# Output projection of the first layer in f16 halves, with scales made on the chip

## The chip, the core and the metric

The kernel runs on one core of one Trainium2 chip. The metric is the device time of one launch in microseconds (us). TensorE is PE in what follows, its weight loads PEld, VectorE is DVE, ScalarE is ACT, GpSimd is POOL and SyncE is SP; in this kernel SP issues all the transfers (DMA) of the part that is changed. Each engine works through its own list of instructions in order, and semaphores tie the lists together.

## The reference, cut to what matters

Three residual layers with a layer norm behind each. Only the first is touched: a short convolution over time, a long one with a kernel as long as the sequence, a gate, and the output projection. Sizes there: 16 time steps, 256 batch rows, 512 channels, all f32.

```python
up = jnp.einsum('lbd,ed->lbe', xn, W_in) + b_in               # xn: layer norm of x, no gain
uc = short_conv(up, short_w) + short_b                        # 3 taps, each channel by itself
x0, x1, v = jnp.split(uc, 3, axis=1)
v = v * x1
y = long_conv(v, k) + v * conv_bias[None, :, None]            # by FFT in the reference
y = y * x0                                                    # the mixed values
y = jnp.einsum('bld,ed->ble', y, W_out)                       # the output projection
x = _layernorm(x + y, axis=-1)                                # x1, which the later layers read
```

## The kernel before

**Stages.** The batch is taken in two halves of 128 rows (`hf` 0 and 1). A half has 24 *slots* (s = 0 to 23) and then 16 *output blocks* (R = 0 to 15 in the first half, 16 to 31 in the second), one for each time step. The 512 channels are four groups of 128 (`cc` 0 to 3), and a slot is one of three kinds (X1, V, X0) of one group for eight of the 16 steps.

**A slot** goes through three engines. PE makes the input projection in f16 halves: 24 matmuls of 128x512 into one of two banks (L574), high times high, low times high, high times low. ACT reads the bank twice, into `u` (L761) and, times the last tap, into `conv_all` (L769). DVE adds the other two taps (L906); a V slot has a product with X1 behind it (L913). ACT may write `u` again only when DVE is done with the slot that read it.

**The long convolution** of a group (`convolve`, L595) is 16 f32 matmuls on PE with a block Toeplitz matrix, behind slots 7, 13, 18 and 22. What it reads is stored by SP to memory and brought back in another layout; its result goes through ACT (`copy_conv`) and again through memory into the tile `y`. `make_y` (L920) then multiplies four tiles of 128x512 of `y` by X0 on DVE: behind slots 9 and 15, half each behind 20 and 21, and the last group's behind the loop.

**An output block** (`out_part`, L616) is four f32 matmuls of 128x512, one for each group, which the profile counts as eight instructions. DVE adds the residual (L926), takes the statistics (L928, L930), POOL makes the reciprocal root, DVE normalises (L935), and SP stores the block (L321) and loads the residual of a block that is seven further on (L316); that load waits for the store of the block that had the buffer, of eight. Blocks 0 to 3 of a half have the first three groups done for all of them before the fourth group. Between the first half's blocks stand the transposes and splits of the second half's x. `LATE` = 8: the second half's last eight blocks do not stand in this loop. Seven of them are threaded into the start of the *heads*, the second layer, from 434 us on.

**In the first half's slots** much is prepared beside them. DVE takes the row maxima of the next group of input weights (`measure_w_in`, L973 to L988, behind slots 1, 6, 11), PE turns the weights (behind slots 4, 9, 14), ACT copies their high halves, DVE takes the low halves ahead of slots 4, 9 and 14 (`split_w_lo`, L993). The output weights are turned on PE behind slot 5, and ACT copies them into `wout_t` as f32 (`copy_w_out`). POOL has the reciprocal roots and little else.

**In the second half's slots** ACT squares eight parts of the feed-forward weights (L800, behind slots 1, 3, 5 and so on), each waiting for a load, and rounds some of them (L814). A row maximum is taken on DVE behind slot 6, turned on PE behind slot 9, reduced on DVE behind slot 10 (L1029) and spread by a small matmul behind slot 11 (L668).

**The order** on each engine is written out by hand: loops over slots, with tables that say behind which slot a piece of other work goes.

```python
SQUARE_AT = {1: 0, 3: 1, 5: 2, 8: 3, 10: 4, 12: 5, 15: 6, 17: 7}
TURN_AT = {4: 1, 9: 2, 14: 3}
MEASURE_AT = {1: 1, 6: 2, 11: 3}
```

SP too has one list: a load that waits holds every transfer behind it.

## Time and profile before

| | |
|---|---|
| time, median of 3 runs | 997.69 us (995.42 to 998.8) |
| the profiled execution | 998.75 us, of which the span is 997.0 us |
| PE busy | 937.2 us, 94% of the span |
| DVE busy | 816.0 us, 82% |
| ACT busy | 632.5 us, 63% |
| POOL busy | 543.1 us, 54% |
| first half's slots, to about | 188 us |
| first half's output blocks, to about | 266 us |
| second half's slots, to about | 403 us |
| heads and what is behind them | 430 us to the end |

The stage times are read from the timelines of PE and SP. In a row of a timeline stand the start and the length in us, the engine, the line, the operation, what it writes and reads, the count, and in brackets the idle time of the engine ahead of it with what ended that. A row of the chain of waits has start, length, and what was on the chain. Busy shares are means over stages that have different limits, so they say little about any one stage.

### The profile page before, as it was taken

Reading aid. Unit: us, or ns where it says so; the run is one execution under the profiler, and the core shown is the slowest. Engines: PE = TensorE matmul, PEld = TensorE weight load, DVE = VectorE, ACT = ScalarE, POOL = GpSimd, SP = SyncE. Lnnn points to the kernel's source line nnn. Section 1 sums busy time; section 2 is a strip of 40 time slices with the busy share of each in tenths; the row PEclk is TensorE's granted clock in tenths of the full one; section 3 lists DMA queues with packets and bytes.
Section 4 is the critical chain, followed back from the end, with each engine's and each line's share of the span. In section 5 each row is a group of like instructions: output and inputs, shape, how many; then the busy total and the mean of one; then the engine's idle time right before and its main releaser. Section 6 shows DMA issues by size and latency. Waiting matters only on the chain.

```text
span 997.0 us, 14896 instructions
## 1 busy us (share of the span) xinstructions
PE 937.2 (94%) x4490; PEld 545.7 (55%) x4490; DVE 816.0 (82%) x1650; ACT 632.5 (63%) x783; POOL 543.1 (54%) x823
## 2 busy tenths in 40 slices
PE   3989999899889999989999999999999999999985
PEld 2545544555335544445566666666666666666641
DVE  6877986399357476687999999999999999999982
ACT  4756545332356565761577777877777787777774
POOL 5302310033100000157888989889898989889851
PEclk9999999899999999999999999999999999999998
DMA  9235677456756657876386876757575665758433
GB/s 320 56 90 154 191 241 234 157 179 205 235 175 211 191 199 253 279 200 198 109 174 135 160 157 137 178 121 182 129 170 142 150 162 130 177 121 188 84 74 85
DMA packets 210268, 167.86 MB, mean 168 GB/s; under 512 B 125861, under 2 KB 166857, under 8 KB 208169
## 3 DMA queue, kind: packets, MB, share of 16 engines
q1 hardware_dynamic: 210216, 167.24, 61.9%
q8 instruction: 25, 0.41, 0.2%
q14 instruction: 27, 0.21, 0.1%
HBM read 112.36 MB, written 33.87 MB: 147 GB/s over the span
## 4 chain that ended last, share of the span: by engine, by line
PE 66%; DVE 14%; DMA 9%; ACT 5%; issue 4%; SPq 2%; DVEq 0%; POOL 0%; POOLq 0%; ACTq 0%
PE conv_bank L1549 17%; PE slot_bank L574 14%; PE hq_bank L1635 11%; PE conv_bank L1559 6%; PE back_bank L1656 4%; PE ff_bank L1656 4%; DMA x_scratch<-res 4%; PE slot_bank L616 4%; DVE conv_all L906 3%; PE conv_bank L595 3%; PE back_bank L1624 1%; PE back_bank L1544 1%; DMA v_ct<-v_scratch 1%; ACT conv_all L769 1%; DVE x_lo L894 1%
## 5 line engine op out<-in xcount | busy, mean ns | idle before, releaser
L906 DVE SCALAR_TENSOR_TENSOR conv_all<-u,taps,conv_all 128x1024 f32<-128x1024 f32 x92 | 122.4, 1331 | 104.2 <-ACT conv_all L769 102.4
L2002 POOL TENSOR_TENSOR sum<-z 128x512 f32<-128x512 f32 x128 | 162.9, 1273 | 23.6 <-DVE z L1865 23.6
L1635 PE MATMUL hq_bank<-x_lo,hq_t 128*128 128x512 f16 x512 | 121.9, 383 | 4.0 <-DMA hq_t<-hq_int 4.0
L616 PE MATMUL slot_bank<-wout_t,y 128*128 128x512 f32 x256 | 114.0, 600 | 3.7 <-DVE res L926 3.7
L761 ACT ACTIVATE u<-slot_bank,bias,unscale 128x1024 f32<-128x1024 f32 x46 | 55.4, 1205 | 94.5 <-PE slot_bank L574 68.7
L2006 POOL TENSOR_TENSOR sum<-sum 128x256 f32<-128x256 f32 x128 | 94.7, 740 | 10.0
L574 PE MATMUL slot_bank<-x_hi,w_hi 128*128 128x512 f16 x384 | 93.1, 385 | 7.5 <-ACT conv_all L769 5.9
L574 PE MATMUL slot_bank<-x_lo,w_hi 128*128 128x512 f16 x384 | 92.5, 383 | 3.0 <-DVE x_lo L894 3.0
L574 PE MATMUL slot_bank<-x_hi,w_lo 128*128 128x512 f16 x384 | 91.9, 382 | 0.0
L1744 ACT ACTIVATE hq_f<-g,h_scale 128x1024 f32<-128x1024 f32 x64 | 73.2, 1144 | 23.5 <-DVE h_scale L1913 19.5
L1918 DVE TENSOR_REDUCE g_max<-g 128x1 f32<-128x512 f32 x128 | 83.9, 676 | 4.8 <-ACT g L1783 4.8
L1549 PE MATMUL conv_bank<-block_diag 128*128 128x288 f32 x324 | 86.4, 407 | 0.1
L1865 DVE TENSOR_TENSOR z<-conv_bank,qx 128x512 f32<-128x512 f32 x128 | 86.3, 674 | 0.0
L1549 PE MATMUL conv_bank<-kv,block_diag 128*128 128x288 f32 x320 | 85.6, 406 | 0.6 <-ACT conv_bank L1735 0.6
L1635 PEld LDWEIGHTS hq_bank<-x_lo,hq_t 128*128 128x128 f16 x512 | 50.4, 99 | 59.6 <-DMA hq_t<-hq_int 4.5
L1168 POOL TENSOR_SCALAR r_rstd<-r_meanvar 128x1 f32<-128x1 f32 x32 | 18.5, 578 | 115.9 <-DVE r_meanvar L930 115.9
L616 PEld LDWEIGHTS slot_bank<-wout_t,y 128*128 128x128 f32 x256 | 48.6, 193 | 60.3 <-issue 55.4
L1559 PE MATMUL conv_bank<-kv_hi,block_diag 128*128 128x288 f16 x376 | 77.0, 286 | 1.2 <-DVE z L1865 0.9
L1852 DVE TENSOR_TENSOR z<-conv_bank,qx 128x384 f32<-128x384 f32 x128 | 70.0, 547 | 0.0
L1549 PEld LDWEIGHTS conv_bank<-block_diag 128*128 128x128 f32 x324 | 60.3, 190 | 17.6 <-issue 0.6
L1549 PEld LDWEIGHTS conv_bank<-kv,block_diag 128*128 128x128 f32 x320 | 59.6, 190 | 17.9 <-ACT conv_bank L1735 1.1
L1656 PE MATMUL ff_bank<-x_hi,xq_t 128*128 128x512 f16 x256 | 65.8, 379 | 3.2 <-ACT g L1783 2.0
(203 smaller groups left out, 1930.1 us busy)
## 6 DMA issues: line engine op xcount, KB each, us to landing
block_diag<-in_ctx_turned SPq DMA_DIRECT2D x32, 512.0 KB, 3.8
x_quad<-in_w_t SPq DMA_DIRECT2D x10, 1024.0 KB, 7.7
stage<-in_ctx SPq DMA_DIRECT2D x16, 512.0 KB, 6.6
v_scratch<-conv_all SPq DMA_DIRECT2D x16, 512.0 KB, 4.1
c_scratch<-v_tok SPq DMA_DIRECT2D x8, 1024.0 KB, 5.3
y<-c_scratch SPq DMA_DIRECT2D x8, 1024.0 KB, 4.9
res<-in_x SPq DMA_DIRECT2D x32, 256.0 KB, 3.2
x_scratch<-res SPq DMA_DIRECT2D x32, 256.0 KB, 3.3
```

Source lines behind the costliest of these rows:

```text
L574: last = nc.tensor.matmul(slot_bank[n % 2][:, q, :], wt[:, dc, e * P:(e + 1) * P], xt[:, dc, cols], start=(j == 0 and dc == 0), stop=(j == ...
L616: last = nc.tensor.matmul(out_bank(R), y[:, cc, t, :], w["wout_t"][:, cc, :], start=(cc == 0), stop=(cc == DC - 1))
L906: ins = nc.vector.scalar_tensor_tensor(out=acc, in0=(u_first[kind] if n < 3 else u)[:, t0 + tap:t0 + tap + T // 2, :].rearrange("p t b -> ...
L1549: last = nc.tensor.matmul(view(conv_bank[tb % 2][:, hh, :], 0, (ROW64, T // 2), (1, PAIRS)), toep[:, head.buf, window * P:(window + 1) * P ...
L1559: last = nc.tensor.matmul(view(conv_bank[tb % 2][:, hh, :], 0, (ROW64, T // 2), (1, PAIRS)), toep_half[:, head.buf, (part * HALVES + windo ...
L1635: last = nc.tensor.matmul(hq_bank[:, :], hq_t[:, fc, :], w["w2_t"][:, fc, :], start=(fc == 0), stop=(fc == FC - 1))
L1656: last = nc.tensor.matmul(bank[:, :], xq_t[:, dc, :], w["w1_t"][:, dc, k * 512:(k + 1) * 512], start=(dc == 0), stop=(dc == DC - 1))
L1744: nc.scalar.activation(hq_f[:, half], g[:, half], ACT.Copy, scale=h_scale[:, 0:1], bias=LOW_HALF).then_inc(hq_rounded, 1)
L1865: nc.vector.tensor_tensor(view(z[:, b, :, :], 0, (SEGS * SEG, T), (2 * SEG + 1, 4), (1, HD)), view(conv, 0, (ROW64, T), (HD, 4), (1, HD)), ...
L1918: nc.vector.tensor_reduce(g_max[:, k:k + 1], g[:, k * 512:(k + 1) * 512], AX_X, ALU.max, apply_absolute_value=True).then_inc(g_maxed, 1)
L2002: nc.gpsimd.tensor_tensor(sum2[:, :, :].rearrange("p t (s j) -> p t s j", j=HD), view(z[:, b, :, :], 0, (SEGS * SEG, T), (SEG, half), (1, ...
L2006: nc.gpsimd.tensor_tensor(sum1[:, :, :], sum2[:, :, 0:2 * HD], sum2[:, :, 2 * HD:4 * HD], ALU.add).then_inc(sum1_done, 1)
```

## The change

The output projection is made from f16 halves. The mixed values are multiplied by a power of two for each channel and split into a high and a low f16 part; the output weights are multiplied by the inverse of that, times one common power of two, and split as well. A block is then three passes of f16 matmuls (high by high, high by low, low by high), 12 instructions of 128x512 in place of 8, and the add of the residual undoes the common scale in the same instruction.

The scale of a channel comes from a bound on its largest value, made in the first half: the sum of the absolute taps and of the absolute long kernel, the sum of the squares of each row of the input weights (`square_rows`), the biases, and a root on POOL. Then the largest of the scaled output weights over all channels is needed, which goes over partitions: DVE takes a maximum for each partition (`top_of_w_out`), PE turns it into a row, DVE takes the row's maximum, PE spreads it with a matmul, DVE makes the scales.

New instructions, beside those that only change their form:

- **Setup, DVE:** five small operations on kernel sums and taps (in `long_kernels`), and `square_rows(0)`, three multiplies of 128x512 with an accumulator, ahead of the first low halves of the weights.
- **First half, DVE:** `square_rows` and `bound_y` (nine small ones) behind slots 4, 6, 8 and 13 (group 0's squares are in the setup), `scale_y` (three small) behind 5, 7, 9 and 14; `top_of_w_out` behind 14, `out_row_of` behind 16, `out_scales` behind 17, `w_out_lo` (four of 128x512) behind 19.
- **First half, PE:** a transpose of the maximum behind slot 15 and a small matmul behind slot 16; the convolution of group 2 waits for the scales. **POOL:** four roots. **ACT:** `w_out_hi`, four copies of 128x512 behind slot 18. **SP:** the load of `y` of group 3 waits for the halves of the output weights, since the turned f32 weights now stand in that part of `y`.
- **Both halves:** `make_y` writes the scaled product into `conv_all`; ACT copies it to f16 (`y_hi`), DVE subtracts that for the low part (`y_lo`), four tiles each, behind slots 9, 16, 21, 22 and the loop. ACT's next X0 slot, and the projection, wait for `y_lo`.
- Some semaphores become one (`rms_steps`, `res_agg`), with the same order of events.

The diff, cut to its core:

```diff
+    BOUND_AT = {4: 0, 6: 1, 8: 2, 13: 3}
+    Y_SCALE_AT = {5: 0, 7: 1, 9: 2, 14: 3}
+    OUT_TOP_AT, TURN_OUT_AT, OUT_ROW_AT, SPREAD_OUT_AT, OUT_SCALE_AT, OUT_HI_AT, OUT_LO_AT = 14, 15, 16, 16, 17, 18, 19
+
+    HI_AT = {9: (0, range(4)), 16: (1, range(4)), 21: (2, range(2)), 22: (2, range(2, 4))}
+    LO_AT = HI_AT
...
+            if k == DC - 1:
+                sp.wait_ge(wout_steps, 13)
...
             for cc in ccs:
-                last = nc.tensor.matmul(out_bank(R), y[:, cc, t, :], w["wout_t"][:, cc, :],
-                                        start=(cc == 0), stop=(cc == DC - 1))
+                for i, (rows, cols) in enumerate(((0, 0), (0, 1), (1, 0))):
+                    last = nc.tensor.matmul(out_bank(R), y_half(cc, t // QUAD, rows, t % QUAD * P, P), wout_half[cols][:, cc, :],
+                                            start=(cc == 0 and i == 0), stop=(cc == DC - 1 and i == 2))
...
+        def turn_out_top():
+
+            pe.wait_ge(wout_steps, 1)
+            pe.wait_ge(ch_copied, 4 * 2)
+            nc.tensor.transpose(turn_bank[3][0:1, 0, :], out_top[:, :], w["ident"][:, :]).then_inc(wout_steps, 1)
+
+        def spread_out_top():
+
+            pe.wait_ge(wout_steps, 3)
+            nc.tensor.matmul(turn_bank[3][:, 1, 0:1], ones[0:1, :], out_row[:, :], start=True, stop=True).then_inc(wout_steps, 1)
...
-                        others = [(w_lo_done, KINDS * (cc + 2))] + [(wout_done, DC)] * (cc == 0)
+                        others = [(w_lo_done, KINDS * (cc + 2))] + [(wout_done, DC)] * (cc == 0) + [(wout_steps, 5)] * (cc == 2)
...
-                act.wait_ge(y_done, 4 * ck - 2 + 2 * pr)
+                act.wait_ge(y_lo_done, 4 * ck - 2 + 2 * pr)
...
+        def w_out_hi():
+
+            act.wait_ge(k_stored, 16)
+            act.wait_ge(wout_steps, 5)
+            for cc in range(DC):
+                nc.scalar.activation(wout_half[0][:, cc, :], wout_f[:, cc, :], ACT.Copy, scale=out_scale[:, cc:cc + 1]).then_inc(wout_steps, 1)
+
+        def y_hi(hf, cc, ks):
+            for k in ks:
+                act.wait_ge(y_done, 4 * (hf * DC + cc) + k + 1)
+                nc.scalar.copy(y_half(cc, k, 0), conv[X0][:, 4 * k:4 * k + 4, :].rearrange("p t b -> p (t b)")).then_inc(y_hi_done, 1)
...
-                out = y[:, cc, 4 * k:4 * k + 4, :]
+                x0 = conv[X0][:, 4 * k:4 * k + 4, :].rearrange("p t b -> p (t b)")
                 dve.wait_ge(c_loaded, 16 * (hf * DC + cc + 1))
-                nc.vector.tensor_tensor(out, out, conv[X0][:, 4 * k:4 * k + 4, :], ALU.mult).then_inc(y_done, 1)
+                nc.vector.scalar_tensor_tensor(out=x0, in0=y[:, cc, 4 * k:4 * k + 4, :].rearrange("p t b -> p (t b)"),
+                                               scalar=y_scale[:, cc:cc + 1], in1=x0, op0=ALU.mult, op1=ALU.mult).then_inc(y_done, 1)
+
+        def y_lo(hf, cc, ks):
+            for k in ks:
+                dve.wait_ge(y_hi_done, 4 * (hf * DC + cc) + k + 1)
+                nc.vector.tensor_tensor(y_half(cc, k, 1), conv[X0][:, 4 * k:4 * k + 4, :].rearrange("p t b -> p (t b)"), y_half(cc, k, 0),
+                                        ALU.subtract).then_inc(y_lo_done, 1)
...
-            nc.vector.tensor_tensor(res[:, i, :], out_bank(R), res[:, i, :], ALU.add).then_inc(res_added, 1)
+            nc.vector.scalar_tensor_tensor(out=res[:, i, :], in0=out_bank(R), scalar=out_unscale[:, 0:1], in1=res[:, i, :],
+                                           op0=ALU.mult, op1=ALU.add).then_inc(res_added, 1)
...
+        def square_rows(i):
+
+            dve.wait_ge(win_scaled, KINDS * (i + 1))
+            for e in range(i * KINDS, (i + 1) * KINDS):
+                link(nc.vector.scalar_tensor_tensor(out=w["wout_t"][:, 0, :], in0=raw_w_in(e), scalar=w["unscale"][:, e:e + 1], in1=raw_w_in(e),
+                                                    op0=ALU.mult, op1=ALU.mult, accum_out=row_squares[:, e:e + 1]))
+
+        def bound_y(i):
+
+            part = slice(i * KINDS, (i + 1) * KINDS)
+            square_of(bias_square[:, part], w["bias"][:, part], REST)
+            link(nc.vector.tensor_tensor(bound[:, part], row_squares[:, part], w["unscale"][:, part], ALU.mult))
+            link(nc.vector.scalar_tensor_tensor(out=bound[:, part], in0=bound[:, part], scalar=MOST * D, in1=bias_square[:, part],
+                                                op0=ALU.mult, op1=ALU.add))
+            link(nc.vector.tensor_tensor(bound[:, part], bound[:, part], tap_sum[:, part], ALU.mult))
+            link(nc.vector.tensor_tensor(bound[:, part], bound[:, part], short_square[:, part], ALU.add))
+            first, second, third = (bound[:, i * KINDS + k:i * KINDS + k + 1] for k in range(KINDS))
+            out = y_bound[:, i:i + 1]
+            link(nc.vector.tensor_tensor(out, first, kernel_sum[:, i:i + 1], ALU.mult))
+            link(nc.vector.tensor_tensor(out, out, second, ALU.mult))
+            link(nc.vector.tensor_tensor(out, out, third, ALU.mult))
+            nc.vector.tensor_scalar(out, out, LEAST, None, ALU.max).then_inc(y_bounds, 1)
...
+        def top_of_w_out():
+
+            dve.wait_ge(wout_done, DC)
+            link(nc.vector.tensor_reduce(out_max[:, :], wout_f, AX_X, ALU.max, apply_absolute_value=True))
+            link(nc.vector.tensor_tensor(out_max[:, :], out_max[:, :], y_pow2[:, :], ALU.mult))
+            nc.vector.tensor_reduce(out_top[:, :], out_max[:, :], AX_X, ALU.max).then_inc(wout_steps, 1)
+
+        def out_row_of():
+
+            dve.wait_ge(wout_steps, 2)
+            nc.vector.tensor_reduce(out_row[:, :], turn_bank[3][0:1, 0, :], AX_X, ALU.max).then_inc(wout_steps, 1)
...
+        def root_of_bound(i):
+            pool.wait_ge(y_bounds, 2 * i + 1)
+            nc.gpsimd.tensor_tensor(y_bound[:, i:i + 1], y_bound[:, i:i + 1], w["neg_half"][:, 0:1], ALU.pow).then_inc(y_bounds, 1)
```

**PE behind slots 15 and 16 of the first half.** Each slot is four rows here, 24 matmuls. Before:

```order
L574 MATMUL slot_bank1<-x_hi,w_lo 128x512 x8
L574 MATMUL slot_bank0<-x_hi,w_hi 128x512 [waits tap2_done,w_lo_done]
L574 MATMUL slot_bank0<-x_hi,w_hi 128x512 x7
L574 MATMUL slot_bank0<-x_lo,w_hi 128x512 x8
L574 MATMUL slot_bank0<-x_hi,w_lo 128x512 x8
L574 MATMUL slot_bank1<-x_hi,w_hi 128x512 [waits tap2_done]
L574 MATMUL slot_bank1<-x_hi,w_hi 128x512 x7
```

Now, with line numbers of the changed kernel:

```order
L611 MATMUL slot_bank1<-x_hi,w_lo 128x512 x8
L694 MATMUL conv_bank1<-ident,out_top 1x128 [waits ch_copied,wout_steps]
L611 MATMUL slot_bank0<-x_hi,w_hi 128x512 [waits tap2_done,w_lo_done]
L611 MATMUL slot_bank0<-x_hi,w_hi 128x512 x7
L611 MATMUL slot_bank0<-x_lo,w_hi 128x512 x8
L611 MATMUL slot_bank0<-x_hi,w_lo 128x512 x8
L699 MATMUL conv_bank1<-out_row,ones 128x1 [waits wout_steps]
L611 MATMUL slot_bank1<-x_hi,w_hi 128x512 [waits tap2_done]
L611 MATMUL slot_bank1<-x_hi,w_hi 128x512 x7
```

The transpose of the maximum (L694) stands between slots 15 and 16, the matmul that spreads it (L699) between 16 and 17, and each waits for a step that DVE makes.

**DVE around slots 13 to 15 of the first half.** Before, from the taps of slot 13 on:

```order
L906 SCALAR_TENSOR_TENSOR conv_all<-u,taps,conv_all 128x1024 [waits tap2_done]
L906 SCALAR_TENSOR_TENSOR conv_all<-u,taps,conv_all 128x1024 [waits tap1_done]
L993 TENSOR_TENSOR w_lo<-conv_bank,w_hi 128x4x128 [waits w_hi_done] x3
L906 SCALAR_TENSOR_TENSOR conv_all<-u,taps,conv_all 128x1024 [waits tap2_done]
L906 SCALAR_TENSOR_TENSOR conv_all<-u,taps,conv_all 128x1024 [waits tap1_done]
L913 TENSOR_TENSOR conv_all<-conv_all 128x1024 [waits conv_done]
L885 TENSOR_SCALAR x_quad<-x_quad,meanvar,rstd 128x512 [waits x_rstd]
```

Now, from the low halves ahead of slot 14 on (ahead of them there are twelve new instructions behind slot 13, squares and bound):

```order
L1070 TENSOR_TENSOR w_lo<-conv_bank,w_hi 128x4x128 [waits w_hi_done] x3
L975 SCALAR_TENSOR_TENSOR conv_all<-u,taps,conv_all 128x1024 [waits tap2_done]
L975 SCALAR_TENSOR_TENSOR conv_all<-u,taps,conv_all 128x1024 [waits tap1_done]
L982 TENSOR_TENSOR conv_all<-conv_all 128x1024 [waits conv_done]
L1117 TENSOR_SCALAR y_scale<-y_bound 128x1 [waits y_bounds]
L1118 TENSOR_SCALAR y_scale<-y_scale 128x1 [waits setup_chain]
L1119 RECIPROCAL y_pow<-y_scale 128x1 [waits setup_chain]
L1124 TENSOR_REDUCE out_max<-y 128x4 [waits wout_done,setup_chain]
L1125 TENSOR_TENSOR out_max<-out_max,y_pow 128x4 [waits setup_chain]
L1126 TENSOR_REDUCE out_top<-out_max 128x1 [waits setup_chain]
L954 TENSOR_SCALAR x_quad<-x_quad,meanvar,rstd 128x512 [waits x_rstd]
```

The maximum over the output weights (L1124 to L1126) stands behind slot 14's product; L694 on PE waits for the last of these. The normalisation of x (L885, now L954) stands behind it.

**DVE at slot 16 of the first half.** Before:

```order
L906 SCALAR_TENSOR_TENSOR conv_all<-u,taps,conv_all 128x1024 [waits tap2_done]
L906 SCALAR_TENSOR_TENSOR conv_all<-u,taps,conv_all 128x1024 [waits tap1_done]
L876 BN_STATS stats<-x_quad 128x6 [waits x_loaded1]
L876 BN_STATS stats<-x_quad 128x6 x3
L879 BN_AGGR meanvar<-stats 128x2 [waits x_stats] x4
```

Now:

```order
L975 SCALAR_TENSOR_TENSOR conv_all<-u,taps,conv_all 128x1024 [waits tap2_done]
L975 SCALAR_TENSOR_TENSOR conv_all<-u,taps,conv_all 128x1024 [waits tap1_done]
L1131 TENSOR_REDUCE out_row<-conv_bank 1x1 [waits wout_steps]
L995 TENSOR_TENSOR y<-conv_all,y 128x512 [waits y_hi_done] x4
L945 BN_STATS stats<-x_quad 128x6 [waits x_loaded1]
```

The row's maximum (L1131), for which L699 on PE waits, stands behind both taps of slot 16, and the four subtractions of group 1 stand behind it.

## Rows read from the trace of the kernel before

**Rows 1.** Chain of waits in order of time: start us, length us, what.

```profile
210.22 3.62 DMA x_scratch<-res
...
446.47 3.43 PE slot_bank L616 x8
...
512.55 1.73 PE hq_bank L1635 x8
```

**Rows 2.** Timeline of DVE, setup: start, length, what, count, idle ahead.

```profile
12.05 0.69 DVE L953 SCALAR_TENSOR_TENSOR block_diag<-x_quad,block_diag 128x512 f32<-128x512 f32 x1
...
18.88 0.17 DVE L973 TENSOR_SCALAR row_max<-row_max 128x3 f32<-128x3 f32 x1
19.08 0.17 DVE L974 TENSOR_SCALAR row_pow<-row_max 128x3 uint32<-128x3 uint32 x1
...
19.82 2.47 DVE L894 TENSOR_TENSOR x_lo<-conv_bank,x_hi 128x512 f16<-128x512 f32 x4
...
24.41 0.16 DVE L986 TENSOR_TENSOR tap_scale<-unscale,taps 128x3 f32<-128x3 f32 x1
24.49 0.15 DVE L987 TENSOR_TENSOR tap_bias<-bias,taps 128x3 f32<-128x3 f32 x1
...
29.85 2.48 DVE L894 TENSOR_TENSOR x_lo<-conv_bank,x_hi 128x512 f16<-128x512 f32 x4 [2.35 <-ACT x_hi L741]
```

**Rows 3.** Windows, DVE: stretch, length, busy (count), clock, DMA share, GB/s.

```profile
57.00:95.00 38.00, 25.79 (x34) 1.00 0.28 76
95.00:133.00 38.00, 35.10 (x50) 1.00 0.71 222
```

**Rows 4.** Timeline of DVE, first half.

```profile
92.38 2.60 DVE L906 SCALAR_TENSOR_TENSOR conv_all<-u,taps,conv_all 128x1024 f32<-128x1024 f32 x2 [5.19 <-ACT conv_all L769]
...
133.07 1.91 DVE L885 TENSOR_SCALAR x_quad<-x_quad,meanvar,rstd 128x512 f32<-128x512 f32 x4
...
137.53 1.23 DVE L913 TENSOR_TENSOR conv_all<-conv_all 128x1024 f32<-128x1024 f32 x1
...
162.43 1.22 DVE L913 TENSOR_TENSOR conv_all<-conv_all 128x1024 f32<-128x1024 f32 x1
...
199.82 0.69 DVE L926 TENSOR_TENSOR res<-slot_bank,res 128x512 f32<-128x512 f32 x1 [2.70 <-PE slot_bank L616]
```

**Rows 5.** Timeline of PE, first half's slots and convolutions.

```profile
54.62 1.04 PE L574 MATMUL slot_bank<-x_lo,w_hi 128*128 128x512 f16 x4 [3.03 <-DVE x_lo L894]
...
131.34 1.89 PE L574 MATMUL slot_bank<-x_hi,w_hi 128*128 128x512 f16 x8
...
136.52 1.89 PE L574 MATMUL slot_bank<-x_hi,w_hi 128*128 128x512 f16 x8
...
148.40 3.84 PE L595 MATMUL conv_bank<-v_ct,block_diag 128*128 128x128 f32 x32 [1.36 <-DMA v_ct<-v_scratch]
...
177.15 6.29 PE L595 MATMUL conv_bank<-v_ct,block_diag 128*128 128x128 f32 x32 [4.20 <-issue]
```

**Rows 6.** Timelines of PE and DVE: slot 21's end, its taps.

```profile
167.61 1.89 PE L574 MATMUL slot_bank<-x_hi,w_hi 128*128 128x512 f16 x8
...
170.15 2.61 DVE L906 SCALAR_TENSOR_TENSOR conv_all<-u,taps,conv_all 128x1024 f32<-128x1024 f32 x2 [1.24 <-ACT conv_all L769]
```

**Rows 7.** Timelines of ACT and PE, second half's slots.

```profile
273.12 1.91 ACT L800 ACTIVATE x_quad<-x_quad 128x2048 f32<-128x2048 f32 x1 [8.24 <-DMA x_quad<-in_w_t]
...
325.69 0.38 PE L668 MATMUL conv_bank<-top_diag,ones 2*128 2x2 f32 x2 [1.34 <-DVE top_diag L1029]
```

**Rows 8.** Timelines, heads' start; last, a window: PE, PEld, DVE, ACT, POOL.

```profile
432.36 2.00 ACT L814 ACTIVATE conv_all<-conv_all,rms 128x2048 f32<-128x2048 f32 x1 [3.13 <-DMA conv_all<-in_w_t]
...
434.13 0.68 DVE L926 TENSOR_TENSOR res<-slot_bank,res 128x512 f32<-128x512 f32 x1
...
434.87 5.40 PE L616 MATMUL slot_bank<-wout_t,y 128*128 128x512 f32 x8 [3.66 <-DVE res L926]
...
443.00:486.00 43.00, 42.85 (x156) 24.76 (x155) 36.32 (x76) 8.26 (x11) 33.32 (x47) 1.00 0.57 168
```

More of the change, by code:

```diff
@@ L859, in scalar_part @@
                     round_part(ROUND_AT[s])
+            y_hi(hf, DC - 1, range(4))
             if hf + 1 < HALF:
@@ L1072, in vector_part @@
         split_lo(0)
+        square_rows(0)
         split_w_lo(0)
@@ L1121, in vector_part @@
             make_y(hf, DC - 1, range(4))
+            y_lo(hf, DC - 1, range(4))
             if not more:
```

137 lines of the change are left out of this document (111 added, 26 removed).

## Prediction

> **What bounds the kernel now.** I read the chain of waits first, for what sets the end in each stretch; then the windows, for how much room VectorE (DVE) has; then the timelines of PE, DVE and ACT around the places that the change touches. The kernel has three kinds of stretch. From 430 us on the heads run, with PE full; the change touches only their start, where seven blocks of the output projection are threaded in. In each half of the batch there are 24 "slots" (input projection and short convolution: 5.18 us of PE, then two ACT steps, then two DVE steps), and behind them 16 output blocks.
>
> Three facts decide. First, one output block is 3.43 us of PE, and eight f16 matmuls of the same size take 1.73, so 12 take 2.59: 0.84 less for each of 32 blocks [rows 1]. Second, in the first half's blocks the chain is not PE but the stores, one behind the other (3.62 each); they hold the next loads on SP, and ACT later sits idle 8.24 us for such a load [rows 1, 7]. Third, in the first half's slots DVE has 12.2 us free in 57–95, but only 2.9 in 95–133 [rows 3]. That is where the change puts its new work.
>
> **Part 1: what PE gives back.** 32 x 0.84 = 26.9 us of PE, but only part is on the path. The first half's blocks are paced by the stores: block 0's add on DVE waited 2.70 for PE [rows 4], and the four new subtractions of the last channel group (2.47 for four [rows 2]) fill just that wait, so the first store leaves as before. I take -1 (ends -3, 0). The second half's first eight blocks end in a wait of PE for DVE (3.66 [rows 8]), so their gain is lost there. The seven late blocks stand in a stretch where PE is busy 42.85 of 43 us and DVE 36.3 [rows 8]: at most -5.9. DVE then has about 1 us of room left, so I take -5 (ends -5.9, -2).
>
> **Part 2: new DVE work in the first half.** Prices [rows 2]: a 128x512 multiply with an accumulator 0.69, with the wait for itself 0.75; small operations that wait for one another 0.20 apart; a subtraction to f16 0.62. So the squares of three weight blocks are 2.25, a bound (nine small ones) 1.8, a scale 0.6, the maximum over 4x512 elements, for which the trace has no row, like a pass of four tiles, 2.5 (1.2 and 4 as ends). The new multiply into conv_all costs what the old one did. The ACT copies of y follow it tile by tile and are priced where they hold something up.
>
> Step 1. The squares of the first weight block (2.25) fit in an idle of 2.35 [rows 2]. The kernel sums (five small operations, 1.0) do not: PE already waits 3.03 us for x_lo behind them [rows 5]. +1.0.
>
> Step 2. Ahead of slot 7, DVE gets bound, scale, squares and bound: 6.5. With step 1 and less 1.4 of idle it ends slot 7 at 93.3 instead of 87.2; the idle of 5.19 ahead of slot 8 [rows 4] is used up. ACT may not overwrite u for slot 8 before, and needs 2.4; slot 8 starts on DVE at 95.8 instead of 92.38: +3.4.
>
> Step 3. From there to 133.07 DVE gets squares and bound twice (8.1), four subtractions (2.5) and a scale (0.6), 11.2, against 2.4 of idle. +12.2: the end of the work at slot 14 moves from 133.07 [rows 4] to 145.3. Then the last scale and the maximum over the output weights: 3.5 with its two small operations. The top is ready at 148.8.
>
> Step 4. **PE waits for it.** The transpose of that maximum stands on PE behind slot 15, which ended at 131.34 [rows 5], and slot 16 stands behind it. PE gets later on the way too (slot 12 now waits for ACT, which waits for the subtractions), by some 9 us, but that is inside this wait. Slot 16 starts at 149.0: +17.7.
>
> Step 5. **A whole round trip is put between two slots.** The matmul that spreads the maximum stands on PE behind slot 16 and waits for a DVE operation that stands behind DVE's part of the same slot 16. From the end of a slot on PE to the end of its DVE part is 167.61 to 172.76, 5.15 [rows 6]; with the reduction (0.3) and the matmul with its hops (0.4, as at 325.69 [rows 7]) PE stands 5.9. Slot 17 starts at 149.0 + 5.2 + 5.9 = 160.1 instead of 136.52 [rows 5]: +23.5. The convolution of channel group 2 then waits for the scales (slot 17's end, 5.15, and six small operations, 1.2): 171.7 instead of 148.40, where it had waited anyway: +23.3.
>
> Step 6. Some comes back. In the trace the convolution of group 3 begins 13.5 us behind its product (163.65 to 177.15 [rows 4, 5]), after a wait of 4.20, and then takes 6.29 where the one before took 3.84; group 2's began 9.6 behind its product (138.76 to 148.40). Now the product is ready at 187.0, PE arrives at 196.1, and the convolution begins at 196.6 to 200.5, at 3.84 without the long wait. The first half's slots end +17 to +23.3 later; I take +19.5, nearer to the shorter way, because the loads that slowed this one are issued earlier relative to it. Wider ends, for DVE prices that I have wrong by a fifth: +11 and +25. Nothing that I see on SP makes this up, since all of the first half's loads and stores move with it.
>
> A row of the trace against a page: small DVE operations that wait for one another start 0.20 apart (18.88, 19.08), and two that do not, 0.08 (24.41, 24.49) [rows 2]. The Trainium skill, page "VectorE: DVE Perf Modes", section "The DRAIN you can't avoid", says that a semaphore between operations costs nothing extra; it measured that on large copies. By that rule some 50 small operations would be 0.1 cheaper, and the time about 5 us lower, near 1012. The row decides here.
>
> **Part 3: the second half and the start of the heads.** ACT's copies of y stand behind slot 9 and wait for the multiply; four subtractions (2.5) stand ahead of DVE's slot 10. The row maximum behind that slot comes 2.9 later, and PE, which had waited 1.34 for it [rows 7], stands that much longer: +2.9 (ends 0, +4.5). The other subtractions there fall into idle of DVE. At the end ACT holds its rounding back until the last copy of y (6 us), and DVE has 2.5 more ahead of its adds. The add at 434.13, which releases PE at 434.87 after 3.66 of waiting, moves by about 3; ACT's idle of 3.13 at 432.36 [rows 8] takes up most of its own delay. PE's next blocks are 0.8 shorter. +2.4 (ends 0, +4).
>
> **Sum,** against the profiled execution's own 998.75 us (span 997.0; the median of the runs shown is 997.69, 1.06 lower): +19.5 - 1 + 2.9 + 2.4 - 5 = +18.8, so 1017.6; less part of that 1.06, I say 1017.
>
> **Rivals.** (a) PE sets the end everywhere, as its busy share suggests: -26.9, 972 us. The stores and the waits on DVE [rows 1, 4, 8] speak against it. The Trainium skill, page "FP8 and Floating Point Precision", section "TensorE Precision Notes", counts four passes for a full f32 product, so three f16 passes save a quarter; the trace agrees on the passes (0.857 against 0.216). It gives this time only where PE is what ends last.
> (b) Faster: the new work in the first half falls into DVE's idle. DVE has 15 us free in 57–133 and more later, against 19 ahead of the top of the output weights; if PE and ACT let DVE run ahead, so that the maximum is there when slot 15 ends and the row maximum when slot 16 ends, the first half costs nothing. Then -1 - 5 + 2.9 + 2.4 gives 998, and 993 if part 3 is hidden as well. The point is the top of the output weights being ready at 131; the trace puts the last product ahead of it at 133.07 without any new work. That speaks against it.
> (c) Steps 2 and 3 are absorbed, and only the two trips remain: the top at 133.07 + 3.5, so +5.3, then +5.9, less some 3 at group 3's convolution: +8 in place of 19.5, 1006 us.
> (d) The change does not do what it says: f16 matmuls whose weights change each time do not run at 0.216 as those of the heads do. The late blocks then give nothing: 1022.
>
> **How the numbers follow.** About 0.3% is what a measurement of this kernel can tell from no change. Forecast, with (d) inside it, 0.70, own range 1010 to 1027; (c) 0.14; (b) at 998 0.06, at 993 0.07; (a) 0.03. So faster 0.10, same 0.06, slower 0.84. The range must hold 8 in 10: 1004 to 1027 takes in (c) and the ends of the unknown costs above it; (a) and (b) are left out.
>
> **What would show it.** In the profile after: the transpose of the output maximum on PE with a wait of some 8 us on DVE, and the matmul behind it with 5 to 6; DVE nearly full from slot 8 to slot 16; the first block's add some 17 us later than 199.82; the gap between the first and last store unchanged; the late blocks at 2.6 us. I am wrong if DVE's reduction over the output weights starts before 140, or if the stores move closer together, since then the first half's blocks give their gain after all.

## The result, and the profile after

The changed kernel takes 1023.0 us (median of 4 runs, 1021.78 to 1024.67), the kernel before 997.41 in the same comparison: a ratio of 1.0244, with a 95% interval of 1.0213 to 1.0275. The profiled execution took 1022.74 us against 998.75, +24.0; its span is 1020.9 us against 997.0, +23.9. The first line of the page after, busy time and share of the span by engine:

```profile
PE 926.8 (91%) x4621; PEld 539.4 (53%) x4621; DVE 862.9 (85%) x1773; ACT 652.5 (64%) x819; POOL 542.8 (53%) x827
```

PE's busy time fell by only 10 us: the matmuls of the blocks take 26.5 us less (114.0 before, 87.5 after), but those of the slots take 10.5 more (277.5 and 288.0), since some of them now ran at half clock. DVE's busy time rose by 47. The blocks are as cheap as they should be. The chain of waits after (start, length, what), to be held against [rows 1]:

```profile
233.48 3.14 DMA x_scratch<-res
...
477.76 2.59 PE slot_bank L654 x12
```

A block takes 2.59 us of PE instead of 3.43: f16 matmuls with changing weights do run at 0.216. The time is lost in the first half. Its timeline of PE:

```profile
55.55 1.45 PE L611 MATMUL slot_bank<-x_lo,w_hi 128*128 128x512 f16 x4 [3.84 <-DVE x_lo L963]
...
115.18 3.57 PE L611 MATMUL slot_bank<-x_hi,w_hi 128*128 128x512 f16 x8 [6.66 <-ACT conv_all L822]
...
148.61 0.37 PE L694 MATMUL conv_bank<-ident,out_top 128*1 128x128 f32 x1 [4.87 <-DVE out_top L1126]
148.78 3.29 PE L611 MATMUL slot_bank<-x_hi,w_hi 128*128 128x512 f16 x8
...
160.75 0.58 PE L699 MATMUL conv_bank<-out_row,ones 1*128 1x1 f32 x2 [5.22 <-DVE out_row L1131]
161.26 3.60 PE L611 MATMUL slot_bank<-x_hi,w_hi 128*128 128x512 f16 x8
...
174.67 3.81 PE L632 MATMUL conv_bank<-v_ct,block_diag 128*128 128x128 f32 x32 [0.91 <-DVE out_scale L1141]
...
201.44 5.44 PE L632 MATMUL conv_bank<-v_ct,block_diag 128*128 128x128 f32 x32 [2.25 <-issue]
```

Three waits for DVE, directly or through ACT, stand where the kernel before has none: 6.66 at slot 12, 4.87 at the transpose of the maximum, 5.22 at the small matmul. Behind each, the first eight matmuls take 3.3 to 3.6 us instead of 1.89. DVE at the places that the prediction named, in its timeline:

```profile
96.20 2.60 DVE L975 SCALAR_TENSOR_TENSOR conv_all<-u,taps,conv_all 128x1024 f32<-128x1024 f32 x2 [2.05 <-ACT conv_all L822]
...
148.40 0.16 DVE L1126 TENSOR_REDUCE out_top<-out_max 128x1 f32<-128x4 f32 x1
...
160.42 0.27 DVE L1131 TENSOR_REDUCE out_row<-conv_bank 1x1 f32<-1x128 f32 x1
...
222.62 0.75 DVE L1002 SCALAR_TENSOR_TENSOR res<-slot_bank,out_unscale,res 128x512 f32<-128x512 f32 x1
```

Its windows, as in [rows 3] (busy, count, granted clock of TensorE, DMA share, GB/s):

```profile
57.00:95.00 38.00, 29.58 (x62) 0.97 0.23 71
95.00:133.00 38.00, 35.83 (x63) 0.87 0.52 170
```

The first add is 22.8 us later than in [rows 4], and nearly all of the change stands there already. This is how the delay against before runs through the program, from the two timelines:

| place | before | after | delay |
|---|---|---|---|
| first half: first add on DVE | 199.82 | 222.62 | +22.8 |
| second half: ACT's first squared part | 273.12 | 295.80 | +22.7 |
| second half: the small matmul behind slot 11 | 325.69 | 349.75 | +24.1 |
| heads: first late block | 434.87 | 459.54 | +24.7 |
| heads: just behind the last late block | 484.08 | 505.15 | +21.1 |
| heads: 10 us further on | 494.11 | 518.10 | +24.0 |
| end of the span | 997.0 | 1020.9 | +23.9 |

### The profile page after: what moved, and what is told of

It is laid out like the page before. It is cut to its first block, busy times and chain, and to the rows that moved or that the text cites. A ratio compares the mean times of both kernels' runs of the same rounds, so it can differ in the third digit from the quotient of the medians.

```text
span 1020.9 us, 15328 instructions
## 1 busy us (share of the span) xinstructions
PE 926.8 (91%) x4621; PEld 539.4 (53%) x4621; DVE 862.9 (85%) x1773; ACT 652.5 (64%) x819; POOL 542.8 (53%) x827
## 4 chain that ended last, share of the span: by engine, by line
PE 57%; DVE 22%; DMA 6%; ACT 4%; issue 3%; SPq 0%; DVEq 0%; POOL 0%; POOLq 0%; ACTq 0%
PE conv_bank L1727 16%; PE slot_bank L611 11%; PE hq_bank L1813 10%; PE conv_bank L1737 6%; DVE conv_all L975 5%; PE back_bank L1834 4%; PE ff_bank L1834 4%; DMA x_scratch<-res 3%; PE conv_bank L632 2%; DVE r_stats L1005 2%; DVE res L1002 1%; PE back_bank L1802 1%; PE back_bank L1722 1%; ACT u L814 1%; DVE z L2043 1%
## 5 line engine op out<-in xcount | busy, mean ns | idle before, releaser
L611 PE MATMUL slot_bank<-x_hi,w_hi 128*128 128x512 f16 x384 | 100.2, 407 | 13.2 <-ACT conv_all L822 11.6
L611 PE MATMUL slot_bank<-x_lo,w_hi 128*128 128x512 f16 x384 | 95.0, 391 | 3.9 <-DVE x_lo L963 3.8
L654 PE MATMUL slot_bank<-wout_t,y 128*128 128x512 f16 x384 | 87.5, 384 | 8.4 <-DVE res L1002 6.6
L1338 POOL TENSOR_SCALAR r_rstd<-r_meanvar 128x1 f32<-128x1 f32 x32 | 18.6, 582 | 120.0 <-DVE r_meanvar L1007 120.0
L611 PEld LDWEIGHTS slot_bank<-x_hi,w_hi 128*128 128x128 f16 x384 | 39.0, 103 | 60.9 <-issue 18.2
L1727 PEld LDWEIGHTS conv_bank<-block_diag 128*128 128x128 f32 x324 | 60.3, 190 | 18.6 <-issue 1.4
L1834 PE MATMUL back_bank<-x_hi,xq_t 128*128 128x512 f16 x256 | 66.1, 381 | 3.5 <-DVE x L2055 3.0
```

The lines of the kernel that those rows point to most:

```text
L611: last = nc.tensor.matmul(slot_bank[n % 2][:, q, :], wt[:, dc, e * P:(e + 1) * P], xt[:, dc, cols], start=(j == 0 and dc == 0), stop=(j == ...
L654: last = nc.tensor.matmul(out_bank(R), y_half(cc, t // QUAD, rows, t % QUAD * P, P), wout_half[cols][:, cc, :], start=(cc == 0 and i == 0) ...
L1727: last = nc.tensor.matmul(view(conv_bank[tb % 2][:, hh, :], 0, (ROW64, T // 2), (1, PAIRS)), toep[:, head.buf, window * P:(window + 1) * P ...
L1834: last = nc.tensor.matmul(bank[:, :], xq_t[:, dc, :], w["w1_t"][:, dc, k * 512:(k + 1) * 512], start=(dc == 0), stop=(dc == DC - 1))
```

## Experiments

Ratios are to the kernel before, with 95% intervals; 0.1% is 1 us. A trace is one execution. Kernels whose code is the same up to the first add have that add up to 1.9 us apart (222.62, 222.96 and 224.50 in the changed kernel, with the store first and with one late pass), so a smaller difference there says little.

### The bound left out

```diff
-        square_rows(0)
-                    if s in BOUND_AT: ...            # and all steps up to out_scales
+        nc.gpsimd.memset(y_scale[:, :], 1.0)
+        nc.gpsimd.memset(out_scale[:, :], 1024.0)
```

> This kernel is the changed one with the bound left out: no sums, squares, roots, no maximum over the output weights and no trip over PE; the scales are fixed powers of two (1 for the mixed values, 1024 for the weights) set by POOL at the start. The f16 halves and the three passes stay. Theory (the bound's work on DVE and its two trips cost the first half's +23.4 us, the halves themselves little): the first add of a block lies within 0 to 3 us of the 199.82 of before, the second half adds 1 to 2, the late blocks give nothing, so 998 to 1004 us. Rival 1 (the copies and subtractions of the halves are what costs): 1012 us or more. Rival 2 (without the bound the 27 us that PE saves come through): 972 to 985 us.

Measured: 1.0058 (1.0036 to 1.0081), about +5.8 us. Three quarters of the loss, 18.6 of 24.4 us, is the bound with its trips; the rest is the halves' own work. Rival 1 falls, since it wanted 1012 us or more, and so does rival 2: without the bound the 27 us of PE still do not come through. The first add stands at 205.00, +5.2, more than the 0 to 3 that I gave it.

### The low part left out as well

```diff
         def y_lo(hf, cc, ks):
-            for k in ks: ...
+            pass
-                for i, (rows, cols) in enumerate(((0, 0), (0, 1), (1, 0))):
+                for i, (rows, cols) in enumerate(((0, 0), (0, 1), (0, 0))):
```

> Fixed scales with the low part of the mixed values left out: no subtractions on DVE (40 in all), and the third pass repeats the first, so that PE's work is the same. Theory (what the halves themselves cost, 5.8 us, is these subtractions in front of DVE's slots and adds): 4 to 7 us less than fixed scales, 996 to 1000. Rival (ACT's copies or the longer add cost it): 1002 to 1005.

Measured: 0.9989 (0.9970 to 1.0007), 6.9 us less than fixed scales: the subtractions on DVE, and the waits for them, are what the halves cost. They are 32, four tiles for each of four groups in both halves, and not 40. The waits of PE, ACT and SP that stood on them now stand on ACT's copies. With the subtractions gone the kernel is where it was, and still not 27 us faster.

### The trip one slot later

```diff
-    OUT_TOP_AT, TURN_OUT_AT, OUT_ROW_AT, SPREAD_OUT_AT, ... = 14, 15, 16, 16, 17, 18, 19
+    OUT_TOP_AT, TURN_OUT_AT, OUT_ROW_AT, SPREAD_OUT_AT, ... = 14, 16, 16, 17, 17, 18, 19
```

> The transpose of the output maximum stands on PE behind slot 16 instead of 15, and the matmul that spreads it behind 17 instead of 16; everything else as in the changed kernel. Theory (PE's two waits, 4.87 and 5.22 us, and the slots at half clock behind them, 1.4 and 1.9 us more, are on the path): both waits go, slot 17 ends near 155 instead of 168.4, and the time falls by 9 to 13 us, to 1010 to 1014. Rival (DVE is so far behind that it sets the end of the slots with or without the trips): a fall of 0 to 3 us, 1020 us or more.

Measured: 1.0153 (1.0120 to 1.0187), 9 us less. But only one wait went. Its timeline of PE:

```profile
148.92 0.27 PE L694 MATMUL conv_bank<-ident,out_top 128*1 128x128 f32 x1
...
159.71 0.58 PE L699 MATMUL conv_bank<-out_row,ones 1*128 1x1 f32 x2 [5.34 <-DVE out_row L1131]
```

The transpose no longer waits. The small matmul does as before, because DVE comes to the row's maximum only behind its part of slot 16, and that was 10.8 us behind the transpose. So the time agreed with the theory for a reason that was half of what I said. In the trace the first add comes 5.7 us earlier (216.93), the first wait and what it did to the clock; the rest of the 9 is inside the interval. The traced execution, 1019.32 us, was the longest of its six.

### The waits filled

```diff
         def turn_out_top():
+            for _ in range(45):
+                nc.tensor.matmul(turn_bank[0][:, 0:2, :]..., w["w_hi"][:, 0, 0:P], x_hi[:, 0, 0:2 * P], start=True, stop=True)
             pe.wait_ge(wout_steps, 1)
...
         def spread_out_top():
+            for _ in range(48):                      # the same matmul
             pe.wait_ge(wout_steps, 3)
```

> The changed kernel with idle PE filled: 45 matmuls of 128x256 into a free bank ahead of the transpose of the output maximum (its wait was 4.87 us), and 48 ahead of the small matmul that spreads it (5.22 us). They use nothing of the result and nothing waits for them. Theory (part of the price of the two waits is that PE runs at the lower clock behind each: slots 16 and 17 took 6.6 and 7.1 us instead of 5.18): both slots go back to 5.2 to 5.4, and the time falls by 2 to 4 us, to 1019 to 1021. Rival (the waits themselves are the whole price, DVE gives the pace behind them): no change, 1023.

Windows of PE over slot 16 and slot 17 (stretch, length, busy, granted clock, DMA share, GB/s), of the changed kernel:

```profile
148.70:155.40 6.70, 6.70 (x25) 0.78 0.05 16
161.20:168.40 7.20, 7.20 (x25) 0.72 0.84 303
```

and with the waits filled:

```profile
148.70:154.00 5.30, 5.30 (x26) 1.00 0.00 0
159.90:165.10 5.20, 5.20 (x26) 1.00 1.05 381
```

The granted clock was 0.78 and 0.72 behind an idle PE, so part of each slot ran at the lower of its two levels (1.2 GHz); behind a busy PE it was 1.00, the higher one (2.4 GHz), and both slots took 5.2 us. Slot 12, where nothing was edited, took 6.6 us here and 8.0 in the changed kernel, behind the same wait of 6.66: what a wait costs behind it differs between executions. The convolution of group 2 began at 171.39 instead of 174.67, 3.3 earlier, and group 3's and the first add (220.36) 1.9 and 2.3 earlier. The time, 1.0226 (1.0198 to 1.0255), lies 1.8 us under the changed kernel's, which the intervals don't tell from nothing. The clock's part of the delay is shown in the trace at group 2's convolution, not in the time.

### The bound taken off DVE, and the trip moved on DVE too

```diff
+        def square_w(i):                             # ACT, blocks 1 to 3, ahead of their scaling
+                nc.scalar.activation(w["wout_t"][...], raw_w_in(e), ACT.Square, accum_out=row_squares[:, e:e + 1])
...
+            after(nc.gpsimd.tensor_tensor(bound[:, part], bound[:, part], tap_sum[:, part], ALU.mult))
+            ...                                      # POOL: the small operations of bound_y
```

> The changed kernel with the bound kept but taken off DVE: the squares of the weight blocks 1 to 3 on ACT (ahead of their scaling), the small operations of the bound on POOL; and the transpose and the small matmul one slot later, as in the second run. DVE keeps the squares of block 0, the kernel sums, the scales, the maximum over the output weights. Theory (what is left of the first half's delay after the two waits is DVE's queue): within 1 to 5 us of fixed scales, 1005 to 1009. Rival (the rest of the delay is the halves' own work or the trips): 1013 to 1017, as with the two steps moved alone.

Measured: 1.0107 (1.0080 to 1.0134), 4.6 us less than the trip moved alone and 4.9 above fixed scales. Its interval and that of the trip moved alone overlap; in the trace the first add came 3.6 us earlier (213.29), so by the trace what DVE was rid of counts. PE's wait at the small matmul was still 5.34, so the next run moved DVE's steps too:

```diff
-    OUT_TOP_AT, TURN_OUT_AT, OUT_ROW_AT, SPREAD_OUT_AT, OUT_SCALE_AT, ... = 14, 16, 16, 17, 17, 18, 19
+    OUT_TOP_AT, TURN_OUT_AT, OUT_ROW_AT, SPREAD_OUT_AT, OUT_SCALE_AT, ... = 14, 16, 15, 17, 16, 18, 19
```

> As with the bound taken off DVE, and DVE's two steps of the trip also one slot earlier: the row's maximum behind slot 15 instead of 16, the scales behind slot 16 instead of 17 (PE's transpose stays behind slot 16, its small matmul behind 17). There PE still waited 5.34 us at the small matmul and ran slot 18 at half clock, since DVE came to the row's maximum only at the end of its part of slot 16. Theory (with DVE's queue and both waits gone the bound is nearly free): the wait of 5.34 goes, 7 to 9 us less than with the bound taken off DVE, 999 to 1003, at or below fixed scales. Rival (the chain through group 3's convolution takes it back): 1006 to 1009.

Measured: 1.0117 (1.0079 to 1.0156), above the theory's range; the rival's 1006 to 1009 lies in the lower part of the interval. The wait went and the time did not. Its timelines of PE and ACT:

```profile
149.71 0.38 PE L703 MATMUL conv_bank<-out_row,ones 1*128 1x1 f32 x2 [0.18 <-DVE out_row L1147]
...
163.43 1.20 ACT L818 ACTIVATE u<-slot_bank,bias,unscale 128x1024 f32<-128x1024 f32 x1 [8.27 <-DVE conv_all L990]
...
190.08 5.44 PE L636 MATMUL conv_bank<-v_ct,block_diag 128*128 128x128 f32 x32 [5.11 <-issue]
```

And a window of DVE:

```profile
136.80:163.40 26.60, 25.98 (x43) 1.00 0.62 220
```

PE waits 0.18 where it waited 5.34. But DVE is busy 25.98 of 26.60 us, so ACT waits 8.27 for it at slot 18, and PE meets its next wait, 5.11 ahead of group 3's convolution. The first add came 2.3 us earlier only (211.03). An idle PE at the trip was, by this run, room that DVE's queue used anyway.

### The store ahead of the load

```diff
-                if R + RES - 1 < HALF * T:
-                    load_res(R + RES - 1)
                 store_res(R)
+                if R + RES - 1 < HALF * T:
+                    load_res(R + RES - 1)
```

The same edit in the changed kernel, in the kernel before, and with fixed scales:

> On SP the store of block R is issued ahead of the load of the residual of block R + 7, so that a store no longer waits behind a load that waits for the store before it; nothing else differs from the changed kernel. Theory (the first half's blocks are paced by that chain, which is why PE's saving there gives nothing): the stores move closer together, ACT's wait for the first squared part near 290 shortens, and the time falls by 8 to 18 us, to 1005 to 1015. Rival (the chain is only what the profile shows as last, and PE or DVE would take its place at once): 1020 to 1023.

> The kernel before, with the one change of the order on SP: the store of block R ahead of the load of the residual of block R + 7. Theory (the chain of stores paces the first half's blocks and holds the load that ACT waits 8.24 us for): that wait goes, PE's waits of 1.83 and 4.09 us at the start of the second half go with it, 988 to 993 us. Rival (the chain matters only together with the halves): 996 to 999.

> Fixed scales, no bound, f16 halves, and the store ahead of the load on SP. Theory (PE's 13 us in the first half's blocks are hidden by the chain of stores): without the chain they show, so the fall against fixed scales alone is larger than that of the kernel before by the same edit, 8 to 14 us: 990 to 996. Rival (once the chain is gone DVE paces these blocks, and PE's saving stays hidden): the same fall as the kernel before has, so that it stays some 6 us above that kernel with the same edit.

| | load first | store first | difference |
|---|---|---|---|
| before | 1 | 0.9937 (0.9911 to 0.9963) | -6.3 us |
| fixed scales | 1.0058 | 0.9960 (0.9940 to 0.9980) | -9.8 us |
| the change | 1.0244 | 1.0155 (1.0118 to 1.0192) | -8.9 us |

The chain of stores was real. From the first half's first store to its last it is 62.3 us in the kernel before (203.45 to 265.74) and 62.6 after (226.37 to 288.94); with the store first it is 50.6 and 50.5, and 49.9 with fixed scales. SP's timeline of the kernel before, first and last store:

```profile
203.45 0.33 SPq L321 DMA_DIRECT2D x_scratch<-res  x1
...
265.74 0.73 SPq L321 DMA_DIRECT2D x_scratch<-res  x1
```

and with the store first:

```profile
204.25 0.33 SPq L321 DMA_DIRECT2D x_scratch<-res  x1
...
254.80 0.33 SPq L321 DMA_DIRECT2D x_scratch<-res  x1
```

PE's saving still does not show. That the two f16 kernels fall by some 3 us more is about what the intervals leave open, and in the traces the stretch from the first add to the small matmul behind slot 11 of the second half is as long in all three: 117.9 us before, 118.0 with fixed scales, 118.4 with the change (load first: 125.9, 128.1 and 127.1). PE does come to the second half's slots 3 us sooner behind the first add with fixed scales (47.6 us against 50.6), and then waits 3 us longer at that matmul (4.41 against 1.34). What stands next in the blocks is in the windows of the two, f32 before and f16 with fixed scales, store first (busy time of PE, PEld, DVE, ACT, POOL):

```profile
204.00:255.00 51.00, 51.00 (x165) 25.28 (x164) 46.33 (x98) 15.11 (x28) 17.78 (x34) 1.00 0.75 253
```

```profile
207.00:257.50 50.50, 43.83 (x219) 23.52 (x218) 47.10 (x98) 14.74 (x28) 17.89 (x34) 0.93 0.77 253
```

With f32 PE is full; with f16 it is not, the stretch is as long, and DVE is busy 93%. DVE is not alone there: in the f16 kernel's chain of waits DVE's adds come first, then a load of the second half's x, for which DVE waits, and behind that PE is the last again.

```profile
215.25 8.58 DMA x_quad<-in_x
...
234.15 10.36 PE slot_bank L654 x48
```

### The late blocks with one pass

```diff
+                passes = ((0, 0), (0, 1), (1, 0)) if R < HALF * T - LATE else ((0, 0),)
```

> The last eight output blocks leave out two of the three passes (high by low and low by high), so each is 0.86 us of PE instead of 2.59. Theory (DVE, not PE, ends last in the stretch where these blocks stand): a fall of 0 to 2 us, 1021 to 1023. Rival (PE is the bound there, and the gain of the first version was lost elsewhere): seven blocks by 1.73 us, 12 us less, 1011.

Measured: 1.0219 (1.0184 to 1.0254), 2.5 us less, inside the intervals. From the first late block to just behind the last it took 45.53 us, and 45.61 in the changed kernel, though each of the eight blocks was 1.73 us of PE shorter. Windows of the stretch, changed kernel and one pass (PE, PEld, DVE, ACT, POOL):

```profile
467.30:509.00 41.70, 39.43 (x193) 23.61 (x194) 38.51 (x76) 8.14 (x11) 33.12 (x48) 1.00 0.56 165
```

```profile
471.00:512.00 41.00, 31.44 (x131) 20.17 (x132) 38.01 (x76) 8.26 (x11) 32.60 (x47) 0.88 0.56 164
```

PE goes from 95% to 77%, DVE stays at 92 to 93%, and PE waits for DVE more often and longer. The longest of these waits, in the timeline of PE with one pass:

```profile
499.53 0.64 PE L1738 MATMUL conv_bank<-kv_hi,block_diag 128*128 128x288 f16 x2 [3.42 <-DVE z L2044]
```

So DVE ends last here. In [rows 8] it was PE, with 42.85 of 43.

### All delays out

The kernel with the bound off DVE and both trips hidden, the store first, and the second half's small matmul one slot later (`SPREAD_AT` 11 to 12); then the maximum over the output weights behind slot 7 instead of 14, and the halves of these weights two slots later.

```diff
-    TOPS_AT, TURN_TOPS_AT, TOP_ROW_AT, SPREAD_AT, ... = 6, 9, 10, 11, 12, 14
+    TOPS_AT, TURN_TOPS_AT, TOP_ROW_AT, SPREAD_AT, ... = 6, 9, 10, 12, 12, 14
```

> The kernel of the run before this one, with the store ahead of the load on SP, and in the second half the small matmul that spreads the row maxima behind slot 12 instead of 11 (PE waited 4.41 us for it with fixed scales, 1.34 in the kernel before). Theory (the three delays add): 9 us less for the stores and 2 to 4 for the matmul, 987 to 993, faster than the kernel before by 0.5 to 1%. Rival (DVE takes over as soon as the stores and the waits are gone): 994 to 999.

```diff
-    ..., OUT_SCALE_AT, OUT_HI_AT, OUT_LO_AT = 14, 16, 15, 17, 16, 18, 19
+    ..., OUT_SCALE_AT, OUT_HI_AT, OUT_LO_AT = 14, 16, 15, 17, 16, 20, 21
...
+                    if s == 7:
+                        out_max_of()
```

> The kernel of the store-first run with the bound (all delays taken out together), with two steps moved: the maximum over each partition of the output weights, 2.28 us of DVE that needs no scale, from behind slot 14 to behind slot 7, where DVE stood idle 5.4 us; and the halves of the output weights two slots later (ACT behind slot 20, DVE behind 21), since ACT's four copies behind slot 18 kept PE waiting 2.2 us. Theory (moving the trip alone gave nothing because DVE was busy 98% of the time from 137 to 163 us and set the pace there): the first add of a block comes 2 to 5 us earlier than in that run, and the time falls by as much, to 990 to 993. Rival (group 3's trip through memory to its convolution sets the pace): no change, 994 to 996.

Measured: 0.9963 (0.9945 to 0.9981) and 0.9967 (0.9948 to 0.9986). Both beat the kernel before, neither by the 0.5 to 1% expected, and the kernel before with the one edit on SP has the lower ratio, 0.9937; the intervals overlap. In the second, group 3's product came 6.4 us earlier (170.27 against 176.71), its convolution 3.5, the first add 2.5 (208.08 against 210.58): DVE's queue was part of the pace, and the trip from the product through memory to the convolution took the rest back. The time of the two is not told apart.

Behind the first add these two are the fastest of all. From that add to the end of the span it is 784.2 and 784.6 us in their traces, 790.0 with fixed scales, 791.6 with the change and 790.5 with the kernel before, all with the store first. Behind that add they differ from the other two f16 kernels only in the small matmul of the second half, whose wait of 4.41 is gone; the traces put some 6 us on it, but it was not run by itself, and not in the kernel before either. What the change still costs stands ahead of that add: 210.58 and 208.08 against 200.62.

## Why the prediction was right, and where its terms were off

The prediction was 1017, with a range of 1004 to 1027; the time is 1023.0. The main mechanism, DVE's new work and two trips over PE in the first half's slots, is as it said. That the sum came as near is in part luck: terms that were too low by 8.5 us met others that were too high by 3.3. By its own steps:

**The chain of step 1 to step 4 held to a fraction of a microsecond.** PE's first matmul behind `x_lo` began at 55.55 instead of 54.62 [rows 5], +0.9 (said: +1.0). DVE's slot 8 began at 96.20 (said: 95.8), the top of the output weights was ready at 148.56 (148.8), slot 16 began at 148.78 (149.0). PE's wait there was 4.87 where I said some 8: PE had got later by more than the 9 that I allowed, because slot 12 ran in part at half clock behind its own wait of 6.66 (8.0 us instead of 5.18), inside this one.

**Step 5: the waits were right, the slots behind them were not.** The wait was 5.22 (said: 5.9). But I priced slots 16 and 17 at 5.18 each behind idle waits of 5 us, and they took 6.6 and 7.1 at a granted clock of 0.78 and 0.72. Group 2's convolution began at 174.67 instead of 171.7. The filled waits give these 3.3 us back at just this place.

**Step 6 gave back less than I took.** Group 3's convolution began at 201.44, behind the later end of 196.6 to 200.5, and took 5.44, not 3.84; I had chosen +19.5 from 17 to 23.3, and the first add shows +22.8. The way from the product to the convolution was 11.6 us, inside the 9.6 to 13.5 of the rows; the product itself was ready 2.9 us later than said (189.9 instead of 187.0), behind the later convolution of group 2. With the waits filled, 2.3 of the 3.3 us come back at the first add. And 23.3, the end of the range, holds only with the old length of 6.29; with the 3.84 that I wrote beside it, the end would have been 20.9.

**Part 1: the first half's blocks gave nothing, for the reason named.** -1 said, -0.1 in the table. The distance of the stores was unchanged, 4.2 us on average (the 3.62 that I named is one of them), and the edit on SP shows that they were the pace. I had not said what stands right behind them. The second half's first eight blocks gave nothing either, as said: PE's wait for DVE at their end, 3.66 in [rows 8], is longer now.

```profile
459.54 4.07 PE L654 MATMUL slot_bank<-wout_t,y 128*128 128x512 f16 x12 [4.99 <-DVE res L1002]
```

**Part 1: the late blocks are the term whose mechanism failed.** -5 said; -3.6 at the last late block, and 10 us later the delay is +24.0 again, so about 0. The rows, before:

```profile
489.99 1.04 PE L1656 MATMUL back_bank<-x_hi,xq_t 128*128 128x512 f16 x4 [0.69 <-DVE x L1877]
```

and after:

```profile
512.84 1.36 PE L1834 MATMUL back_bank<-x_hi,xq_t 128*128 128x512 f16 x4 [2.22 <-DVE x L2055]
```

PE came early and waited for DVE there. DVE's 36.3 of 43 us [rows 8] looked like room; it was work that had only to fit into 5 us less, and it is in a chain with PE (each group's matmuls, then DVE, then PE). Of the 2.9 us lost again here, 1.5 is that longer wait; some 1.1 more is that the matmuls behind it ran in part at the lower clock (granted 0.68 from 512.80 to 518.10; 4.12 us became 5.26). One pass instead of three left the late blocks' stretch as long as it was (45.53 us).

**Part 3 was too dear.** +2.9 and +2.4 said, +1.4 and +0.6 in the table. PE's wait at the small matmul did grow by 3.07, from 1.34 [rows 7] to 4.41, but PE came to it only 21.0 us later than before, not 22.7. And the reason that I gave for it, the subtractions, is wrong at this place: without them the wait was still 4.40. The rows after, of PE, ACT and DVE:

```profile
349.75 0.58 PE L717 MATMUL conv_bank<-top_diag,ones 2*128 2x2 f32 x2 [4.41 <-DVE top_diag L1175]
```

```profile
341.81 2.60 ACT L860 CAST y<-conv_all 128x512 f16<-128x512 f32 x4 [4.60 <-DVE conv_all L989]
```

```profile
346.65 2.61 DVE L975 SCALAR_TENSOR_TENSOR conv_all<-u,taps,conv_all 128x1024 f32<-128x1024 f32 x2 [0.48 <-ACT conv_all L822]
```

ACT waits 4.60 for DVE's multiply, makes its four copies of `y`, and only then reads slot 10's bank, for which DVE waits; without the subtractions DVE waits for it longer, 2.88, to the same end. No run took the copies away by themselves.

The errors of the terms are +3.3 (slots), +0.9 (first half's blocks), -1.5 and -1.8 (part 3) and +4.3 (late blocks): 5.2 us, from 18.8 to the 24.0 of the profiled executions. The largest is the late blocks.

**The rivals.** (a) falls: with all of the bound gone, the ratio is still 1.0058. (b) falls with the top at 148.56 instead of 131, and (c) with slot 8 at 96.20 and the wait of 6.66 at slot 12. (d) falls with 2.59 us for a block; its 1022 is near the time because it, too, takes nothing for the late blocks, but for another reason. On the row against the page: the bound's small operations, each waiting for the one ahead, did start 0.20 apart in the trace after (102.63, 102.83, 103.03), as [rows 2] had it.

**What PE waits for ahead of group 3's convolution.** The profile names nothing for it ("issue"). It was 2.25 to 7.90 us in these kernels, and from the end of the product on DVE to that convolution it took 11.6 us (after) to 14.6 (early maximum). SP's rows name it: the load of what the convolution reads, its issue and its time from issue to landing, after and with the early maximum:

```profile
195.87 0.70 SPq L372 DMA_DIRECT2D v_ct<-v_scratch  x1
DMA to landing us min/median/max: 5.5/5.5/5.5
```

```profile
180.47 0.70 SPq L376 DMA_DIRECT2D v_ct<-v_scratch  x1
DMA to landing us min/median/max: 5.6/5.6/5.6
```

The load lands at 201.4 and 186.1, and the convolution begins at 201.44 and 186.12. Ahead of its issue SP waits for the stores of the product, 5.4 us after and 7.9 with the early maximum: the load is issued 6.0 us behind the end of the product after, and 9.0 with the early maximum. So it is the trip through memory, and the store is the part of it that differs. Why the store took longer there stays open, and no run shortened the trip.

## What to carry to other kernels

A saving on the engine that is 94% busy was worth next to nothing in three stretches (the blocks of the first half, of the second half, and the late ones): a chain of stores or DVE stood right behind it, and the work that made the saving possible went to DVE. Before taking work from one engine, look in each stretch for the second one in line, and price the new work there. A value that goes over partitions and back (reduce, transpose, reduce, spread) made PE wait some 5 us at each hop here, a lag of the pipeline from PE to DVE, because the hop's place in PE's list came before DVE had done its step. Moving the hops back takes such a wait away, but it gives time only where DVE's queue has room: the first move gave 9 us, the second none. And a wait of PE can cost again behind it, through the clock.

## What was not expected of the hardware

PE's clock: after waits of 4.87 and 5.22 us with PE idle, eight f16 matmuls of 128x512 took 3.29 and 3.60 us against 1.89, and the slots of 24 ran at a granted clock of 0.78 and 0.72; with 45 and 48 matmuls of 128x256 in the waits it was 1.00. The Trainium skill, page "TensorE: Matmul & The Clock Gate", section "What's actually happening", gives 1.2 GHz for an array that has been idle and 2.4 GHz for one under load; these rows agree. And an order of two instructions on SP's queue, a store and a load that waits for an older store, was worth 6.3 us in the kernel before; no kernel with the change fell below the kernel before by more than 4.0 us (fixed scales with that same edit), or 3.7 with the bound kept.
